# Retention scores of a macaron block: plain float32 from zero-padded heads on four row groups in place of split sums on two

## The reference, cut to what matters

```python
x = x + 0.5 * ffn(layernorm(x), ...)      # attention, 4 experts
x = x + retention(layernorm(x), ...)      # the part that is changed
x = x + 0.5 * ffn(layernorm(x), ...)
```

```python
q, k, v = split(hidden @ W_qkv)           # 128, 128 and 256 columns
q, k = rotary(q), rotary(k)               # x * cos + swapped(x) * sin
r = einsum('bhtd,bhsd->bhts', q, k) * dk ** -0.5 * decay_mask   # causal
out = einsum('bhts,bhsv->bhtv', r, v)
out = group_norm(out per head) * silu(hidden @ W_g) @ W_proj
```

## Time and profile before

| | us |
|---|---|
| median of 3 runs | 1020.77 (1016.85 to 1021.35) |
| span of the profiled execution | 1029.0 |
| TensorE busy in that span | 879.9 (86%) |
| VectorE | 766.6 (75%) |
| ScalarE | 685.2 (67%) |
| GpSimd | 617.7 (60%) |
| mean granted TensorE clock | 0.952 of 2.4 GHz |

### The profile page before, as it was taken

How to read it: one execution, slowest core, us unless ns; L and a number is a source line. 1 busy time by engine, 2 the same in 40 slices (tenths; PEclk the granted TensorE clock), 3 DMA queues, 4 the chain that set the end, 5 groups by cost and what they waited for, 6 DMA issues and landing times.

```text
span 1029.0 us, 26933 instructions
## 1 busy us (share of the span) xinstructions
PE 879.9 (86%) x8607; PEld 658.9 (64%) x8607; DVE 766.6 (75%) x1936; ACT 685.2 (67%) x1402; POOL 617.7 (60%) x913
## 2 busy tenths in 40 slices
PE   5898999999988785588888898899999999987784
PEld 3565666666656784466666676666666666657784
DVE  5687888888967776365666566578888888887785
ACT  2687888888865675244444444588888888874674
POOL 4144566666636667266767777426575757546666
PEclk9998999999988998699999999799999999998998
DMA  9994992000044673200000000000000000045672
GB/s 304 409 369 58 327 407 110 21 10 20 11 133 129 192 221 99 82 1 1 0 0 0 0 0 1 2 1 12 12 20 10 20 11 20 11 120 174 178 228 72
DMA packets 41958, 97.70 MB, mean 95 GB/s; under 512 B 5240, under 2 KB 25486, under 8 KB 37276
## 3 DMA queue, kind: packets, MB, share of 16 engines
q1 hardware_dynamic: 36380, 84.16, 25.2%
q0 software_dynamic: 5504, 12.63, 3.4%
HBM read 44.68 MB, written 53.13 MB: 95 GB/s over the span
## 4 chain that ended last, share of the span: by engine, by line
PE 44%; DVE 19%; issue 19%; POOL 12%; ACT 2%; DVEq 1%; DMA 1%; POOLq 0%; SPq 0%; ACTq 0%
DVE mx L1385 8%; PE duo L570 8%; PE duo L626 7%; PE duo L563 3%; POOL out L1953 3%; PE duo L862 2%; DVE qk_lo L1374 2%; POOL x_mid L1953 2%; PE duo L848 2%; PE duo L635 2%; PE duo L564 2%; POOL xs L1945 2%; PE duo L892 2%; PE duo L933 2%; DVE ret L1697 1%
## 5 line engine op out<-in xcount | busy, mean ns | idle before, releaser
L1385 DVE TENSOR_REDUCE mx<-duo 128x4 fp32r<-128x1024 f32 x256 | 312.2, 1220 | 72.6 <-PE duo L570 67.4
L1083 ACT ACTIVATE probs<-duo 128x1024 f32<-128x1024 f32 x256 | 262.9, 1028 | 60.4 <-PE duo L576 56.6
L570 PE MATMUL duo<-stacks 32*128 32x256 f32 x1024 | 133.7, 339 | 36.7 <-DVE mx L1385 28.9
L626 PE MATMUL duo<-probs,v_st 128*32 128x256 f32 x2048 | 144.8, 403 | 0.1
L576 PE MATMUL duo<-q_st,stacks 32*128 32x256 f32 x1024 | 132.5, 339 | 0.1
L570 PEld LDWEIGHTS duo<-stacks 32*128 32x128 f32 x1024 | 81.0, 192 | 72.7 <-issue 33.1
L1849 POOL TENSOR_TENSOR a_ln<-mv_ln,eps_ln 128x2 f32<-128x2 f32 x32 | 6.3, 196 | 151.2 <-DVE mv_ln L1350 151.1
L1697 DVE TENSOR_TENSOR ret<-duo,dm 128x768 f32<-128x768 f32 x64 | 61.0, 953 | 47.3 <-PE duo L852 44.5
L563 PE MATMUL duo<-qk_hi,sel_r 128*128 128x256 f32 x256 | 82.5, 343 | 7.1 <-DVE qk_lo L1374 7.1
L626 PEld LDWEIGHTS duo<-probs,v_st 128*32 128x32 f32 x2048 | 55.2, 113 | 43.6 <-issue 7.5
L1224 ACT ACTIVATE stacks<-duo 128x512 fp32r<-128x512 f32 x64 | 38.2, 597 | 66.5 <-PE duo L863 66.5
(11 more groups left out here) (231 smaller groups left out, 2404.1 us busy)
## 6 DMA issues: line engine op xcount, KB each, us to landing
x_sorted<-ret SPq DMA_DIRECT2D x2, 17476.0 KB, 52.8
wbuf<-w_pack SPq DMA_DIRECT2D x38, 512.0 KB
ret<-x_sorted SPq DMA_DIRECT2D x22, 257.0 KB
stacks<-x_sorted SPq DMA_DIRECT2D x12, 257.0 KB
wside<-w_pack SPq DMA_DIRECT2D x38, 66.0 KB
w_pack<-wbuf SPq DMA_DIRECT2D x2, 1024.0 KB, 5.8
decay_rows<-prow SPq DMA_DIRECT2D x1, 1536.0 KB
xs<-x_sorted SPq DMA_DIRECT2D x4, 257.0 KB
```

The lines of the kernel that those rows point to most:

```text
L570: return pe.matmul(score_bank[h % 2][:, t * SEQ:(t + 1) * SEQ], q_st[r:r + 32, g, t * P:(t + 1) * P], k_st[r:r + 32, g, :], start=True, st ...
L626: last = pe.matmul(pv_bank[32 * j:32 * j + 32, cols], v_st[:, t, h, :], probs[:, h % RING, t, :], start=(t == 0), stop=(t == TT - 1))
L1083: act.activation(probs[:, h % RING:h % RING + 2, :, :], duo_now[:].rearrange("p (n t q) -> p n t q", n=2, t=TT), ACT.Exp, scale=SCALE).the ...
L1385: dve.tensor_reduce(rows, score_duo[:].rearrange("p (n t k) -> p n t k", n=2, t=TT), AX.X, ALU.max, negate=True).then_inc(max_done, 1)
```

## The change

- The columns of `W_qkv` for queries and keys and the rotary tables are reordered on the host (`spread_heads`), so that heads 2j and 2j+1 lie on the 32 rows of group j.
- `sel2_r`, its load of 1 MB and its conversion, `qk_hi`, `qk_lo` and the rounding of values are removed. The expansion and its ScalarE copies are removed.
- ScalarE makes, from `qk`, one copy of the queries and two of the keys, each times a 0/1 column (`parity`) that blanks the other head of each 32 rows (`part_heads`).
- `scores` does four heads at a time in plain float32, one on each of four groups of 32 rows, into banks 0 to 3. `mask_scores` stays at one instruction for two heads.
- `weigh` writes both groups of four heads into one bank (6), and one ScalarE copy of 128x512 takes both. Banks are dealt out anew; the PSUM of gates and of the output is bank 4.
- The order in every engine's body, and every line of the seam, is new. The statistics of the input run three batches ahead instead of two; `body` starts at -3.

```diff
-    def scores(g):
-        pe.wait_ge(rex_ready, i * 4 + g + 1)
-        wait(pe, ret_ready, i * 4 + g)
-        for n in range(2):
-            r = 64 * n
-            pe.matmul(bank[n][:, 0:256], r_st[r:r + 64, g, 1, 0:P], r_st[r:r + 64, g, 0, :], ...)
-        for n in range(2):
-            r = 64 * n
-            last = pe.matmul(bank[n][:, 256:384], r_st[r:r + 64, g, 1, P:2 * P], r_st[r:r + 64, g, 0, P:2 * P], ...)
+    def scores(b, n):
+        pe.wait_ge(heads_ready, b * 3 + 2 + n)
+        wait(pe, ret_ready, b * 4 + 2 * n)
+        for j in range(4):
+            rows_j = slice(32 * j, 32 * j + 32)
+            pe.matmul(bank[j][:, 0:256], k_heads[rows_j, n, 0:P], q_heads[rows_j, :], start=True, stop=True)
+        for j in range(4):
+            rows_j = slice(32 * j, 32 * j + 32)
+            last = pe.matmul(bank[j][:, 256:384], k_heads[rows_j, n, P:2 * P], q_heads[rows_j, P:2 * P], ...)
         last.then_inc(rs_ps, 1)
```

TensorE, one body (each step only where its batch is live):

```diff
+    0 queries_keys(i + 1)   # wait rT_ready; second half: wait rv_ready, b
+    1 out_to_tokens(i - 1)  # wait oT_ready
+    2 scores(i, 1)
+    3 gates(i + 1)          # wait xr_done, i - 2
+    4 weigh(i, 0)           # wait ret_ready 4i+2, rv_ready i+1, on_ready i
+    5 weigh(i, 1)           # wait ret_ready 4i+4
+    6 scores(i + 1, 0)      # wait heads_ready, ret_ready 4i+4
+    7 gated_to_dims(i - 2)  # wait yr_ready, gz_ready i+2
+    8 values(i + 1)         # wait rot_ready (bank 5)
+    9 to_dims(i + 2)
+    10 project(i - 2)
```

ScalarE and VectorE:

```diff
+    def part_heads(b):
+        act.wait_ge(rqk_ready, b + 1)
+        wait(act, rs_ps, b * 2)
+        act.activation(q_heads[:], qk[:, 0, :], ACT.Copy).then_inc(heads_ready, 1)
+        for n in range(2):
+            act.activation(k_heads[:, n, :], qk[:, 1, :], ACT.Copy, scale=parity[:, n:n + 1]).then_inc(heads_ready, 1)
+    # ScalarE: out_tokens(i-1), gate_tanh(i+1), part_heads(i+1), out_heads(i),
+    #          out_gated(i-2), out_values(i+1), out_dims(i+2)
+    def out_dims(b):
+        act.wait_ge(rT_ps, b + 1)
+        wait(act, rv_ps, b)
+        wait(act, z_ps, b)
+        act.activation(sT[:], bank[7][:, 0:SEQ], ACT.Copy).then_inc(rT_ready, 1)
+    # VectorE: mask_scores(i,0), (i,1); add_output(i-3); sum_squares(i-1);
+    #          rotate(i+1); mask_scores(i,2), (i,3); gate(i+1); normalized(i+2);
+    #          statistics(i+3); group_normalized(i-1); aggregate(i+3)
```

GpSimd and the seam of TensorE:

```diff
     def body(i):
-        gated(i); use_values(1); rsqrt("rln", i + 2); add, round, subtract of i + 1; rsqrt("gn", i - 1); use_values(0)
+        gated(i - 2); add_rotated(i + 1); rsqrt("gn", i - 1); rsqrt("rln", i + 3)

-    retain(BATCH - 1, slots(0, 3))
+    retain(BATCH - 1, slots(1, 2))
     attend(BATCH - 1, slots(0, 2))
     retain(BATCH - 1, slots(4, 4))
+    retain(BATCH - 1, slots(7, 7))
     attend(BATCH - 1, slots(3, 5))
-    retain(BATCH - 1, slots(5, 7))
+    retain(BATCH - 1, slots(5, 5))
+    retain(BATCH - 1, slots(10, 10))
+    retain(BATCH, slots(1, 1))
     attend(BATCH - 1, slots(6, 7))
-    retain(BATCH, slots(0, 1))
     attend(BATCH, slots(0, 0))
-    retain(BATCH, slots(2, 3))
+    retain(BATCH, slots(7, 7))
     attend(BATCH, slots(1, 2))
-    retain(BATCH, slots(4, 4))
+    retain(BATCH, slots(10, 10))
     attend(BATCH, slots(3, 3))
-    retain(BATCH, slots(5, 7))
-    retain(BATCH + 1, slots(0, 4))
+    retain(BATCH + 1, slots(7, 7))
     attend(BATCH, slots(4, 4))
-    retain(BATCH + 1, slots(5, 7))
+    retain(BATCH + 1, slots(10, 10))
     attend(BATCH, slots(5, 7))
```

More of the change, by code:

```diff
@@ new lines, in values, with to_dims @@
+                def values(b):
+                    pe.wait_ge(rot_ready, b * 2 + 2)
+                    for t in range(TT):
+                        last = pe.matmul(bank[5][:, t * SEQ:(t + 1) * SEQ], sT[:, t * P:(t + 1) * P], wv_cen[:], start=True, stop=True)
+                    last.then_inc(rv_ps, 1)
+                def to_dims(b):
+                    pe.wait_ge(rln, b * 8 + 8)
+                    wait(pe, rot_ready, b * 2 - 1)
+                    for t in range(TT):
+                        last = pe.transpose(bank[7][:, t * P:(t + 1) * P], s_nat[:, t, :], ident[:])
+                    last.then_inc(rT_ps, 1)
@@ new lines, in project, with body @@
+                def project(b):
+                    pe.wait_ge(yT_ready, b + 1)
+                    for t in range(TT):
+                        for half in range(2):
+                            last = pe.matmul(output_bank(b)[:, t * P:(t + 1) * P], yT[:, half, t * P:(t + 1) * P], wproj[:, half, :],
+                                             start=(half == 0), stop=(half == 1))
+                    last.then_inc(pr_ps, 1)
+                def body(i, part=range(11)):
+                    for s in part:
+                        if s == 0 and live(i + 1, 0):
+                            queries_keys(i + 1)
+                        elif s == 1 and live(i - 1, 0):
+                            out_to_tokens(i - 1)
+                        elif s == 2 and live(i, 0):
+                            scores(i, 1)
+                        elif s == 3 and live(i + 1, 0):
+                            gates(i + 1)
+                        elif s == 4 and live(i, 0):
+                            weigh(i, 0)
+                        elif s == 5 and live(i, 0):
+                            weigh(i, 1)
+                        elif s == 6 and live(i + 1, 0):
+                            scores(i + 1, 0)
+                        elif s == 7 and live(i - 2, 0):
+                            gated_to_dims(i - 2)
+                        elif s == 8 and live(i + 1, 0):
+                            values(i + 1)
+                        elif s == 9 and live(i + 2, 0):
+                            to_dims(i + 2)
+                        elif s == 10 and live(i - 2, 0):
+                            project(i - 2)
```

488 lines of the change are left out of this document (196 added, 292 removed).

## The result

The changed kernel took 988.44 us (median of 4 runs, 983.06 to 990.3) against 1021.06 for the kernel before (4 runs). The ratio is 0.9662, 95% interval 0.9633 to 0.9691. A second series on another chip, beside eleven runs of the kernel before, gave 0.9657 (0.9609 to 0.9705).

The account below looks back on a forecast made before the run. TensorE's work was taken to bound the kernel before, a ring of waits the new one. Savings of 31.0 + 0.6 + 4 = 35.6 us from 1029.0 gave 993.4, scaled to 986; forecast range 975 to 997.

Parts of the forecast that it names:

- 15 batches x 2.07: Retention stage: 2.07 us saved in each of 15 batches, 31.0 us in all.
- clock and filling: Retention stage: lower clock and filling cost 0.33 us a batch before; kept in proportion, 0.6 us less in all.
- seam: Last queries and keys to attention's sixth slot of scores: 36.2 us before, 32 after, 4 us less taken.
- The ring's 11.16: Retention batch: a circle of waits across TensorE, ScalarE, VectorE and GpSimd, its terms summing to 11.16 us.
- burst 0.83: TensorE's score matmuls for four heads, plain float32 on four overlapping row groups: 0.83 us, start and layout change included.
- The "tie" of the two branches: After rotation: masks and `weigh` on one branch, 2.61 us, against 2.67 over GpSimd and ScalarE.
- the 2.5 us of removed TensorE work: TensorE in one retention batch: 4.2 us removed, 1.7 added, 2.5 net, of which 2.07 come through.
- the rival: Retention stage: TensorE's new gap makes the clock fall to 1.2 GHz, up to 1051 us; chance 0.07.
- the extra 0.2 us by the rule: Score burst: with the 3.07 speedup plus start and layout change, 1.03 us, every batch 0.2 longer, about 3 in all.
- The longer ring: Retention batch: slower bursts, dearer head copies and late hops make 12.1 us a batch, 1000 us; chance 0.12.
- the serial bursts: Score bursts: row groups don't overlap, 2.6 us each, 13.0 to 13.3 a batch, 1014 to 1020 us; chance 0.06.

Follow-up runs that it names:

- the second profile: The changed kernel run again unchanged, on the chip of other follow-up runs: ratio to the kernel before 0.9657, 11.09 us a batch.
- the run with the root first: Changed kernel with GpSimd's inverse root of batch 14 put in front of the normalisation of attention's first inputs: 993.4 us, seam 42.3 us.
- GpSimd's steps back: Changed kernel with useless GpSimd work the size of the removed rounding and subtraction before the sum, batches 0 to 12: 1023.9 us, 12.75 to 12.77 a batch.
- one row group: Changed kernel with all four matmuls of a score burst reading rows 0 to 31: 1049 us, 13.22 to 13.33 a batch at full clock.
- the gap filled: Changed kernel with four useless matmuls before `weigh(b, 1)` in the first 13 batches: ratio to the kernel before 0.9634, 11.13 us a batch.
- one exchange of two steps on VectorE: Changed kernel with `sum_squares` moved behind the rotation in VectorE's body: median 966.7 us, ratio to the kernel before 0.9428, 9.92 a batch.

## Why the prediction was right

**The number.** 986 was forecast, 988.4 measured, inside 975 to 997. Its largest term, 15 batches x 2.07, was right for the reason given, and a little small: 15 x (13.27 - 11.09) = 32.7. That the sum fits is in part luck, for errors cancel: stage with clock and filling 31.6 forecast and 34.3 measured, seam 4 and 1.8 (35.6 and -0.9 in the second profile). The ring's 11.16 was measured at 11.09, and single terms fit: burst 0.83 against 0.86; masks behind the rotation 1.81 against 0.87 + 0.95; ScalarE's query copy 0.42 against the 0.50 taken, each key copy 0.49 against 0.60, both taken a little dear. The "tie" of the two branches hid a slip: 0.87 + 0.95 + 0.14 + 0.57 + 0.22 is 2.75 and not 2.61, so the prediction's own terms put the masks' branch in front, by 0.08 us. Measured it is in front by 0.18, and it is the one that binds.

**What bounds the kernel before.** This step failed in part: "TensorE's own work bounds, and what is taken from it counts until another ring of waits takes over." I read it from a chain that was mostly TensorE. But "one mask of VectorE between" left out what the same chain has in front of the next `gates`:

```profile
573.72 0.61 ACT att_pair L1234
...
575.05 0.42 DVE xs L1735
```

From 573.62 to 575.52, where `gates` begins, it is ScalarE's squares, their sum and the adding of the output, 1.9 us, and with the mask 3 us of the batch are not TensorE. Taking 0.92 us off TensorE in the kernel before gave 0.55 at full clock and almost nothing over the stage. Two waits for VectorE, the gate that frees bank 7 and the mask behind the rotation, stood within 0.1 us behind that chain; a chain of what ended last doesn't show how close the next one is, the timelines of the engines do. The forecast survived since the sum was not made of removed work but of the new ring's own terms against 13.27 measured. Had I forecast the 2.5 us of removed TensorE work, the size would have looked about right too, for the wrong reason.

**What comes through.** The removal of two GpSimd steps between rotation and scores is enough to account for 1.7 us a batch (12.76 back to 11.09), 25 us in 15 batches. This run can't say what the old order would have made of the same removal; the new order without the rest of the change wasn't tried.

**The seam.** 4 us were taken, 1.8 measured in the first profile, -0.9 in the second. The step that failed is that the split and expansion of attention's first batch would end near 20 us after the last queries and keys: the expansion ended at 21.0, and the first slot began, behind ScalarE's copies, at 603.91 - 582.06 = 21.85. Scaling of batch 14 waits for GpSimd's inverse root, and that stands behind attention's first normalisation in GpSimd's queue, which I hadn't counted. VectorE first, then GpSimd:

```profile
595.05 0.68 DVE L1693 TENSOR_REDUCE ssq<-att_pair 128x16 f32<-128x512 f32 x1
...
594.74 1.58 POOL L1836 TENSOR_SCALAR s_nat<-xs,mv_prep,rstd_prep 128x128 f32<-128x128 f32 x2 [0.20 <-POOL rstd_prep L1829]
...
597.09 0.22 POOL L1961 TENSOR_TENSOR ra_gn<-ssq,eps_gn 128x16 f32<-128x16 f32 x1
597.39 2.93 POOL L1963 TENSOR_TENSOR v_gn<-ra_gn,half_root 128x16 f32<-128x16 f32 x1
```

The root's input is there at 595.7, and GpSimd turns to it 1.4 us later (the expectation of the run with the root first had 3.5). Putting the root first costs more than it gives, for attention's first slot then waits for the normalisation: both stand on GpSimd, and from 587.1 to 600.3 the chain that ended last is almost all GpSimd. What the best order of the seam is stays open. The other runs with this seam and the four row groups took 33.8 to 37.3 us for it, so one profile doesn't tell 34.6 from the 36.4 before.

**The clock.** "I keep them in proportion" was near: clock and filling cost 4.8 us before (203.8 - 15 x 13.27) and 3.2 after, 1.6 less where 0.6 was taken. A fall in the steady part costs 1.6 us where the earlier trace rows had 1.5. That the clock falls more often in some orders is real, but the gap alone didn't bring it. The 4.7 us that the rival adds to a batch at the lower clock is a slip too: its terms give 4.3, or 5.1 with `weigh`. In two kernels in which the ring was longer by slow work elsewhere (GpSimd's steps back, one row group) the stage's clock stood at 0.86 and 0.84; in those with the gap filled, shortened or closed it stood at 0.96 to 0.98, with the gap as it was at 0.93 and 0.94.

**The rivals.** The Trainium skill, "TensorE: Matmul & The Clock Gate", section "Measured speedup vs the span model", gives 3.07 for four row tiles. Here one row group took 2.81 us and four took 0.86, a factor of 3.3, starts and layout changes included; my 0.83 left those in as well, so the extra 0.2 us by the rule didn't come. The page's figure is for 512 columns a matmul, these have 256 and 128. The longer ring and the serial bursts did not occur; one row group shows that the second's price (13.0 to 13.3 a batch) was right at full clock, at its upper end, and that the falling clock would have put it at 1049 us, on the slower side, and not at 1014 to 1020 as I had it.

## What to carry to other kernels

A pipeline of one body over several engines is timed by its ring: write down, with durations from the old trace, what each queue holds in front of each waiting instruction, and sum it; shares of busy time and the amount of work removed don't give that number. Look for a waiting instruction that stands in a queue before one whose input is already there: here one exchange of two steps on VectorE was worth 22 us, two thirds of what the whole rewrite had won. Then ask of each step that is moved away what wait it had been covering. And where the clock falls in every batch, compare two points between which it is full, or the clock's loss is taken for the edit's.

## What the runs showed of the hardware

- Plain float32 matmuls of 32 rows on four row groups overlap: 0.86 us for four heads, 2.81 on one group.
- With TensorE's idle 1.8 us a batch filled with useless full-array matmuls the granted clock stood at 2.4 GHz from 426 to 600 us (one profile). The same stage of the changed kernel had two and three falls to 1.2 GHz. In these runs the useless work cost 0.04 us a batch, the falls 1.6 us each.
- With the bursts on one row group the stage was granted 0.84 of the clock while the profile has TensorE busy for 98% of it, with no wait over 0.54 us behind the first 20; the changed kernel had 0.93 and 84%. Why the first was lower wasn't tried.
- The kernel before was granted 0.94 over its stage, and 0.90 with eight matmuls a batch left out.
- GpSimd's inverse root of 128x16 takes 2.9 us, of 128x2 0.7.
